# A graph layer's opening loads, a narrower tile window and a shorter count sum

## What is computed

```python
edge_index = jnp.stack([src, dst])
h = jnp.maximum(_layernorm(x, axis=-1), 0.0)          # 12500 x 128
# inside the layer, with z = h:
agg = segment_sum(z[src], dst) / maximum(deg, 1.0)
h = relu(agg @ Wg + z @ Ws + bg)                      # 128 -> 128
h = tanh(h @ W1 + b1)                                 # 128 -> 512
h = tanh(h @ W2 + b2)                                 # 512 -> 512
out = x + h @ W3 + b3                                 # 512 -> 128
```

## Time and profile before

| | |
|---|---|
| median of 3 runs | 1374.68 us |
| the profiled execution | 1376.32 us |
| its span in the trace | 1374.2 us |
| PE busy | 1244.6 us, 91% |
| VectorE busy | 1068.2 us, 78% |
| ScalarE busy | 675.5 us, 49% |
| GpSimd busy | 699.7 us, 51% |

### The profile page before, as it was taken

How to read it: one execution, slowest core, us unless ns; L and a number is a source line. 1 busy time by engine, 2 the same in 40 slices (tenths; PEclk the granted TensorE clock), 3 DMA queues, 4 the chain that set the end, 5 groups by cost and what they waited for, 6 DMA issues and landing times.

```text
span 1374.2 us, 28936 instructions
## 1 busy us (share of the span) xinstructions
PE 1244.6 (91%) x10456; PEld 966.7 (70%) x10456; DVE 1068.2 (78%) x1973; ACT 675.5 (49%) x1389; POOL 699.7 (51%) x749
## 2 busy tenths in 40 slices
PE   1118999999999999999999999999999999999998
PEld 1015767777777767777777777777777677777777
DVE  5898899778878868887788788877877887788640
ACT  4904555446445525554464355535544554465343
POOL 1156544565556545555555545556555445565500
PEclk9558999999999999999999999999999999999999
DMA  9743322332333233313313332233133123323300
GB/s 208 223 141 92 99 66 62 109 114 50 103 108 100 54 105 97 105 47 112 111 44 108 108 94 78 72 109 106 48 110 113 49 76 110 113 60 92 112 16 12
DMA packets 72969, 128.47 MB, mean 93 GB/s; under 512 B 17584, under 2 KB 55854, under 8 KB 68126
## 3 DMA queue, kind: packets, MB, share of 16 engines
q1 hardware_dynamic: 49774, 78.31, 18.2%
q0 software_dynamic: 22784, 46.71, 13.1%
q10 hardware_dynamic: 274, 1.60, 0.5%
HBM read 113.41 MB, written 13.15 MB: 92 GB/s over the span
## 4 chain that ended last, share of the span: by engine, by line
PE 82%; DVE 9%; ACT 4%; issue 3%; DMA 2%; DVEq 0%; ACTq 0%
PE banks L828 25%; PE banks L774 21%; PE banks L790 11%; PE banks L697 7%; PE banks L842 6%; PE banks L811 4%; PE banks L800 2%; PE banks L747 2%; DMA ring<-in_dst_dram 2%; PE banks L803 2%; DVE arena L1496 1%; ACT arena L1041 1%; PE banks L856 1%; DVE arena L1506 1%; DVE mean_rows L1535 1%
## 5 line engine op out<-in xcount | busy, mean ns | idle before, releaser
L623 POOL DMA_INDIRECT ring<-h_table,idx_all x712 | 687.1, 965 | 562.0 <-issue 217.9
L1124 ACT CAST arena<-banks 128x512 f16<-128x512 f32 x675 | 373.5, 588 | 140.9 <-PE banks L774 134.0
L828 PE MATMUL banks<-dense,w 128*128 128x256 f32 (+1 forms) x1568 | 417.3, 383 | 0.2
L774 PE MATMUL banks<-xin,arena 125*128 125x256 f16 x2700 | 372.2, 274 | 26.2 <-DVE arena L1496 24.7
L774 PEld LDWEIGHTS banks<-xin,arena 125*128 125x128 f16 x2700 | 248.3, 98 | 110.6 <-issue 25.1
L828 PEld LDWEIGHTS banks<-dense,w 128*128 128x128 f32 x1568 | 262.4, 191 | 35.2 <-ACT dense L1101 8.0
L1506 DVE TENSOR_TENSOR arena<-node,banks 128x768 f16<-128x768 f16 x216 | 198.4, 980 | 5.7 <-PE banks L790 5.7
L1496 DVE TENSOR_SCALAR arena<-arena,code_ptr 128x768 f16<-128x768 f16 (+1 forms) x432 | 181.1, 482 | 15.0 <-PE banks L774 13.1
L790 PE MATMUL banks<-arena 64*128 64x257 f16 x2700 | 164.0, 272 | 6.2 <-DVE arena L1506 5.5
L697 PE MATMUL banks<-ring,onehot 128*128 (+1 forms) x836 | 159.2, 275 | 0.0
L790 PEld LDWEIGHTS banks<-arena 64*128 64x128 f16 x2700 | 126.9, 95 | 41.3 <-issue 13.0
(11 more groups left out here) (122 smaller groups left out, 929.6 us busy)
## 6 DMA issues: line engine op xcount, KB each, us to landing
arena<-unit_codes SPq DMA_DIRECT2D x27, 1600.0 KB
ring<-h_table,idx_all POOLq DMA_INDIRECT x712, 2.6
tblk<-h_table SPq DMA_DIRECT2D x48, 128.0 KB
xblk<-in_x_dram SPq DMA_DIRECT2D x48, 128.0 KB
out_dram<-dense SPq DMA_DIRECT2D x48, 128.0 KB
xin<-in_x_dram SPq DMA_DIRECT2D x5, 1120.0 KB
h_table<-xin SPq DMA_DIRECT2D x5, 1120.0 KB
w<-in_L_gnn_W_dram SPq DMA_DIRECT2D x1, 1024.0 KB, 6.3
```

The lines of the kernel that those rows point to most:

```text
L623: nc.gpsimd.indirect_dma_start(out=ring_tiles[:, t % RING, 0:2 * D], out_offset=None, in_=table, in_offset=bass.IndirectOffsetOnAxis(ap=id ...
L774: mm = nc.tensor.matmul(to, wide_l[0:TP, piece % WSLOTS, k, j, :], tab[0:TP, row_of(g, j), :], start=(j == 0), stop=(j == 1))
L828: mm = nc.tensor.matmul(l3_ps[c][:, 0:w], w2[:, q, c * P:(c + 1) * P], h2T[:, q, 0:w], start=(q == 0), stop=(q == HC - 1))
L1124: nc.scalar.copy(unit_msgs[:, 2 * pr:2 * pr + wide_of, 0:2 * D], unit_ps[pr % 2][:, 0:wide_of * 2 * D].rearrange("p (g d) -> p g d", d=2 * ...
```

## The change

Edge lists: SyncE now issues them, behind the third chunk of `x`; ScalarE casts them after chunk 1 instead of 0 and takes `dst` after chunk 2 instead of 1; VectorE takes `idx` after `norm_shift(3)`. GpSimd scales 8 rows of a chunk, ScalarE 12. A step sums 18 tiles, and its window may begin up to 22 tiles in. The counts of a unit are added once more, tiles 4 to 7 onto 0 to 3, in a second VectorE instruction that waits for the first, so that 5 matmuls are left.

```diff
-POOL_ROWS = 5
+POOL_ROWS = 8
-LOT_NS = 1520
+LOT_NS = 1505
-W = 19
-REACH = 21
+W = 18
+REACH = 22
+CQ = TH // 4
+COUNTED = [*range(CQ), *range(2 * CQ, TH // 2)]
...
             for c in range(TC):
                 for lo, hi in SPREAD:
                     sp.dma_start(xin[lo:hi, c * ROWS:(c + 1) * ROWS], x_chunk[c, lo:hi]).then_inc(x_in[c], 16)
+                if c == 2:
+                    for k, (a, s) in enumerate(((src, src_in), (dst, dst_in))):
+                        sp.wait_ge(stage_padded, k + 1)
+                        sp.dma_start(stage_rows[0:FULLQ, k], a[0:E - ODD].rearrange("(q e) -> q e", e=STRIP)).then_inc(s, 16)
+                        sp.dma_start(stage_rows[FULLQ:FULLQ + 1, k, 0:ODD], a[E - ODD:E].rearrange("(q e) -> q e", q=1)
+                                     ).then_inc(s, 16)
...
             def carry_groups(n):
-                pe.wait_ge(group_count_ready, n + 1)
+                pe.wait_ge(group_count_ready, 2 * (n + 1))
                 at(pe, oblk_ready, PLACE[PERIODS[n - 1][1][0]] if n > 1 else 0)
-                for t in range(TH // 2):
-                    mm = nc.tensor.matmul(carry_ps, before16[:], group_count[:, :, t], start=(t == 0), stop=(t == TH // 2 - 1))
+                for t in COUNTED:
+                    mm = nc.tensor.matmul(carry_ps, before16[:], group_count[:, :, t], start=(t == COUNTED[0]),
+                                          stop=(t == COUNTED[-1]))
...
-                if c == 0:
+                if c == 1:
                     cast_stage()
-                if c == 1:
+                if c == 2:
                     take_dst()
...
                 nc.vector.tensor_tensor(counted, hits_by_count[:, :, 0], hits_by_count[:, :, 1], ALU.add
                                         ).then_inc(group_count_ready, 1)
+                dve.wait_ge(group_count_ready, 2 * n + 1)
+                nc.vector.tensor_tensor(counted[:, :, 0:CQ * HG], counted[:, :, 0:CQ * HG], counted[:, :, CQ * HG:2 * CQ * HG],
+                                        ALU.add).then_inc(group_count_ready, 1)
...
                 norm_stats(c + 1)
-                if c == 2:
-                    take_idx()
                 if c:
                     norm_low(c - 1)
                 norm_shift(c + 1)
+                if c == 2:
+                    take_idx()
```

More of the change, by code:

```diff
@@ L1020, in _ @@
         def _(act):
[L1021 to L1025, removed]
             def norm_sdev(c):
```

## The result

The changed kernel takes 1364.42 us (median of 5 runs, 1363.29 to 1367.35), the kernel before 1376.14 us beside it. The ratio is 0.9918, with an interval of 0.9895 to 0.9941: 11.7 us less, where 12.0 were forecast. The forecast time was 1362.7 us. The profiled execution's span went from 1374.2 to 1362.6 us.

The account below looks back on a forecast made before the run. PE (TensorE) was taken to bound the kernel from about 210 us on, with loads, ScalarE and VectorE setting the opening. Steps -4.4, carry -4.3, one-hots -0.4, second addition +1.1, opening -4.0: -12.0 us, to 1362.7 us; range 1356 to 1369.

Parts of the forecast that it names:

- a period that shortens by other than 0.4 us: Sign of being wrong, in normal periods: 48.7 us were forecast to become 48.3 us.
- Steps: TensorE's 44 steps lose one tile's matmul each, 0.10 us apiece, all on PE's path: -4.4 us.
- one-hots: VectorE's one-hot matrices shrink from 19 to 18 tiles; on its path in the opening and period 2: -0.4 us.
- Carry: TensorE's carry has five matmuls instead of nine, 0.178 us less in each of 24 units: -4.3 us.
- Second addition: VectorE's extra addition of counts, 0.41 us with its wait, hidden in normal periods: +1.1 us in opening and period 1.
- piece 6: Tightest VectorE comparison for PE in a normal period: 2.0 us of slack still cover the second addition, no new wait.
- The 0.3 us put down to period 1: First piece matched behind the count in period 1: 0.14 us of slack against 0.41 leaves +0.3 us.
- Opening: Later lists and shorter ScalarE scaling let VectorE start chunk 3 at 34.6 us instead of 37.98: -4.0 us with square-root waits.
- Both waits for the square root: VectorE's two opening waits of 0.33 us each for ScalarE's square root go, as the shorter scaling ends in time.
- one half clock more: Rival: period 1's new wait of 0.3 us tips PE to half clock, 1.5 us more, 1364.2 us; chance 0.07.
- The pace of the gathers: LOT_NS, the modelled time between gathers, falls by 1%; effect zero, bounded by 1.3 us on either side.

Follow-up runs that it names:

- v_late11: Changed kernel with one tile of the run behind dense layer 2 kept back to stand between layers 2 and 3; 1364.08 us, ratio 0.9895 to the kernel before.
- u_window2: Changed kernel with 19 tiles in a step's span and a reach of 21 again; 1366.99 us, ratio 0.9935 to the kernel before.
- a_copy: The changed kernel run again with no edit; 1366.10 us, ratio 0.9914 to the kernel before.
- u_carry2: Changed kernel with nine carry matmuls and no second addition, as before; 1368.31 us, ratio 0.9940 to the kernel before.
- u_open: Changed kernel with its opening as before: early lists on ScalarE's queue, casts behind chunk 0, five rows on GpSimd; 1371.07 us, ratio 0.9955 to the kernel before.
- u_loads: Changed kernel with edge lists back on ScalarE's queue at the start, GpSimd keeping 8 rows; 1458.81 us, ratio 0.9954 to the kernel before at 1465.14 us.

## Why the forecast was right, and where its terms were not

The sign and the size held, and so did the mechanism of the carry, of the addition and of the opening. The mechanism of the steps did not, and that the sum came within 0.3 us is luck: the steps gave some 2 to 3 us less than their term and the opening 1 to 1.5 us more. The prediction named "a period that shortens by other than 0.4 us" as a sign of being wrong, and that sign is there: 0.20. Cut by place, the 11.6 us between the two spans are 6.2 up to the end of unit 0 (forecast 3.3), 3.4 in the 17 normal periods (forecast 6.5) and 2.0 in the rest.

- **Steps (-4.4, with the one-hots -4.8): failed.** "All are on PE's path" is the sentence that is wrong. The price of a tile, 0.10 us, is right where nothing hides it (v_late11 against u_window2). In the changed kernel the second step's is given back in the wait for ScalarE's tanh (0.11 us a period), and the alternating issue gap takes about 0.1 us a period more. Measured: nothing in normal periods, 1.9 us in five others, where the one-hots' 0.14 us is part of it; 2.9 us by the ratio, with an uncertainty of 2.6.
- **Carry (-4.3): right.** 0.22 us for five matmuls, 0.19 us a period.
  An estimate by the price of 81 ns that the Trainium skill's page "TensorE: Matmul & The Clock Gate", section "Back-to-back issue gap", has for a sustained pair at 128 columns gives 7.8 us. The five matmuls of 100 columns in 0.22 us are 44 ns each, as before, and the period's 0.19 us bears that out; the measurement decides.
- **Second addition (+1.1): right in size,** as far as it can be seen. 375 ns, no new wait at piece 6, VectorE's slack at the end of a unit still 2.02 us (302.69 us), and TensorE's wait at the first gather still 0.58 us in 19 of 22 cases. The 0.3 us put down to period 1 did not come. It stands in a unit alone further on: in period 9, now at full clock, TensorE waits 0.39 us at the first gather (at 502.08 us), and the same 0.39 is in a_copy three times, each in a unit alone at full clock. Without the addition such a unit shows no wait: period 15 of the kernel before (791.19 us) and period 2 of u_carry2 (170.02 us). They are the only two at full clock to compare; in u_carry2 the clock fell in the other three.
- **Opening (-4.0): right mechanism, too small.** Chunk 3 was begun at 33.34 us and not at 34.6. The landing rate was the term: with 217 GB/s forecast, 226 GB/s were moved on the mean (6.72 MB in 29.7 us behind the lead of 3.6). This is partly the chance of a trace: all ten of this order have 31.95 to 35.14 us, with a mean of 33.8, and 34.6 lies within them. Both waits for the square root went, 0.83 us in place of the 0.66 forecast. The gain is 5.5 us in the first trace, 5.0 over the ten (last `norm_low` at 64.4 us on the mean against 69.42) and 5.6 by the ratio of u_open.
- **The clock** was a rival with one half clock more. In fact they moved. Period 9 fell before and not after, period 15 the other way, seen at the 8 matmuls of layer 2:
```profile
499.70 1.99 PE L820 MATMUL banks<-dense,w 128*128 128x256 f32 x8 [0.56 <-ACT dense L1097]
...
778.62 3.78 PE L820 MATMUL banks<-dense,w 128*128 128x256 f32 x8 [0.56 <-ACT dense L1097]
```
The eight take 1.8 us more, and the period 2.5 us, where I had priced 1.5. Here -2.52 and +2.49 us cancel. In 125:135 us the granted clock was 0.83 before and 1.00 after; unit 0 ends 6.2 us earlier in the first trace of the changed kernel and 3.7 in a_copy's, so such steps move single traces by 2 us and more.

The ratios close: u_open 5.6, u_carry2 3.6 and u_window2 2.9 us are 12.1 us, where a_copy has 11.9. Each is uncertain by 2.6 us, so that the close agreement proves little. The pace of the gathers was not tried alone; no wait of TensorE for a gather shows in either trace.

## What to carry to other kernels

A matmul taken from a busy TensorE is worth its time only where nothing behind it waits for another engine's answer to what stood ahead of it. Look at each place it is taken from: in a chain matmul, activation, matmul the independent tiles between the two are the cover of that wait, and taking one out moved nothing here. The better use of such tiles is to place them where the rows show a bracket: moving seven tiles was worth more here than the whole change.

## Not expected of the hardware

- One issue gap of 0.2 us in every second period, at the last of eight tiles, appears with 18 tiles and not with 19 or with a run of seven or five. What decides it is open: no run varied the stream of instructions alone.
- The landing of chunk 3 moved by 3.2 us from trace to trace of kernels with the same order of loads, at a busy share of the DMA engines of about 1 in each.
- In one round the kernel before took 1465 us instead of 1376, though the opening was as fast (chunk 3 begun at 32.5 to 34.5 us in the traces of the new order). Where TensorE gathers, it waits for ScalarE's copies and its own issue; of the whole trace of u_loads:
```profile
PE banks L777 <- DVE arena L1502: 32.3, 24, 10.3
PE banks L777 <- ACT arena L1127: 29.6, 54, 1.5
...
PE banks L777 <- issue: 12.3, 18, 1.7
```
The columns are us in total, times, longest. In the changed kernel's first trace the same matmuls wait 25.0 us for VectorE, 23 times, and the other two rows are not there. The copies themselves take 0.59 us in both. Why the answers come later is not settled; that round and a later one with 1376.62 us have the same chip number.
